# A decoder layer on one core: new instruction orders for start, middle and end, grouped moments, bias rows by TensorE

## The chip, the cores and the metric

One core of a Trainium2 chip. The time is that of one launch on the device in microseconds (us); the median of several runs counts. A profile of one execution gives the span from the first to the last instruction of the core and every instruction's start and duration.

## What is computed

One decoder layer over 32 batch items (here "batches") of 128 tokens and 128 features, 16 heads of 8. Cut to what matters:

```python
x = x + self_attn(layernorm(layernorm(x)) * ln_g + ln_b)   # scores + relative bias, softmax, @ w_out + b_out
x = x + cross_attn(layernorm(x), ctx, mask)                # masked softmax, @ Wo + bo
x = x + ffn(layernorm(x))   # y, h rounded to 8 bits per row, ternary weights; h = silu(gate) * up, then down
```

Scores need more accuracy than bf16 gives, so queries and keys are split into three bf16 parts each (their sum is the float), and the nine products stand as rows of one contraction.

## The kernel before, in words

The kernel is one program for five engines, each with its own list of instructions in fixed order; semaphores tie them together. There is no loop on the chip: Python runs a function `step` for t = -1 to 41 (`STEPS`, L41) and each call adds to every engine's list the instructions of that step. A helper such as `scores_a("X", st, 5, 1)` takes the stage (S self-attention, X cross-attention, F feed-forward), a lag and a chunk: in step t it works on batch t - 5, and does nothing if there is no such batch (`Step.of`). The order of the lines in each engine's `step` is the order of its work; one such list serves all 43 steps, and where work is missing at the start and the end, what is left keeps its place. `run(step)` (L216) drives it.

What happens to one batch, stage S:

- DVE: `ln_stats`, `ln_moments` (bn_stats, bn_aggr of x, L785 and L795), GpSimd (POOL): `variance`, `negate_mean`, `inverse_std`, `normalise` (L404 to L436) give xn.
- TensorE (PE): `xn_transposed`; ScalarE (ACT): `xnT_out`; PE: `project_qkv`; ACT: `qk_out` (the two bias columns), `part1`, `part2`, `v_out`; POOL: `rest`, `part3`. This makes the bf16 parts.
- SP's queue: `parts_again` and `parts_out` write the parts to a DRAM scratch, `stack_in` (L305, L308) reads them back as `stack_q` and `stack_k`, two buffers each (`STACKS`). For S the lower rows of the stack hold the relative bias; `rel_rows` (L235) fills them once for buffer 0, from ACT's queue for stack_k and SP's for stack_q, and `rel_copies` (L244) copies them to buffer 1. `scores_a` of batch 0 waits for the first, of batch 1 for the second.
- `scores_a` (PE, L1128) makes the scores in four chunks of four heads, in two PSUM banks; `row_max` (DVE; L900 for S, one reduction a chunk, L895 for X, four masked ones a chunk) takes the negated maxima; POOL splits them (`max_hi`, `max_lo`), PE transposes, ACT copies, and `max_in` (SP, L319) puts them as two more rows under `stack_q`.
- `scores_b` (PE, L1148) makes the transposed scores less the maximum, `exp` (ACT, L599) the probabilities, `attend` (PE, L1166) sums values and denominators; `o_raw_out`, `o_transposed`, `attend_sums`, `attend_norm` (DVE, L910, L920), `on_transposed`, `oT_out`, `project_out` (PE, L1245), `residual` (DVE, L930). Before that, POOL's `add_shift` (L458) has added the output bias row (with the values' bias carried through w_out) to x.

Stage X is the same with ctx as keys and values. Stage F: moments and xn on POOL as above, `y_max`, `y_unit`, `y_inverse` (DVE, L958), `quantise_y` (POOL), `y_transposed`, `yT_out`, `gate_up` (PE), `tanh` (ACT, L711), `gate` and `gated` (DVE, L965 and L975: h), `h_max`, `h_quantum`, `h_inverse`, `h_scaling`, `quantise_h` (ACT, L721), `h_transposed`, `hT_out` (ACT, L659), `down`, `residual_ffn` (L1027). Rounding adds 1536 in 16-bit floats; `yT_out` and `hT_out` take it off with a bias column.

PSUM banks are shared: bank_t by `o_transposed`, `gate_up`, `h_transposed`, `down`; bank_s by the small transposes and `project_out`; bank_p by `project_qkv` and `gate_up`; bank_o by `attend`. Who must have read a bank before it is written again stands by hand as arguments of each PE helper, as in

```python
scores_a("S", st, 2, 3, ("max_S", 2, 2), ("max_X", 6, 4), ("max_X", 6, 2), ("max_S", 3, 4))
```

SP's list also holds the bulk loads (`bulk_load`, L330 to L337): ctx and mask of four batches, and x of four batches two groups ahead, each 256 KB in a step of its own; x of batches 0 to 7 is loaded at the very start.

Of the kernel before, what the change touches and what calls it, by code (L numbers as in the profile page):

```python
# [16 lines left out]
CH = 4  # L28
HC = H // CH
# [11 lines left out]
STEPS = [(t, t) for t in range(-1, B + 10)]  # L41
# [4 lines left out]
CTX_TURN, MASK_TURN, X_TURN = 0, 2, 1  # L46

ONES, IDENT, V_AUG_S, POOL_CONST = 2, 5, 14, 17
SCALED, QK_BIAS, REL_SPLIT, V_BIAS, DVE_CONST = 1, 6, 12, 15, 17
ABS_SUM, MEAN_W, FFN_CONST = 1, 2, 15  # L50
# [7 lines left out]
class Step:  # L58


    def __init__(self, s, x):
        self.first = {"S": s, "X": x, "F": x}

    def of(self, stage, lag):

        first = self.first[stage]
        return first - lag if first is not None and 0 <= first - lag < B else None


START = Step(0, None)  # L70


def layer(nc, x, ctx, mask, w_self, w_cross, w_ffn, w_down, cols, w_out_s, w_out_x, bo_rows,
          rel_w, rel_const, scratch, scratch_rel, out):
    es = ExitStack()
    with es:
# [11 lines left out]
        w_tern = sb("w_tern", [D, 3, F], BF16)  # L88
        col = sb("col", [D, CONST_COLS])
        bo = sb("bo", [S, 2, D])  # L90
        shift = {"S": sb("shift_s", [S, D]), "X": sb("shift_x", [S, D])}
# [8 lines left out]
        round16 = sb("round16", [128, 1])  # L100
        minus_round16 = sb("minus_round16", [128, 1])
        y_step2 = sb("y_step2", [S, 1])
        minus_half = sb("minus_half", [128, 1])
# [22 lines left out]
        stats = {k: sb(f"stats_{k}", [S, 6]) for k in "SXF"}  # L126
        mv = {k: sb(f"mv_{k}", [S, 2]) for k in "SXF"}
        veps = {k: sb(f"veps_{k}", [S, 1]) for k in "SXF"}
        rstd = {k: sb(f"rstd_{k}", [S, 1]) for k in "SXF"}
# [8 lines left out]
        probs = {a: sb(f"probs_{a}", [S, CH, HC * S]) for a in "SX"}  # L138
        o_raw = {a: sb(f"o_raw_{a}", [128, 2, S]) for a in "SX"}
        neg_mean = {k: sb(f"neg_mean_{k}", [S, 1]) for k in "SXF"}  # L140
# [21 lines left out]
        hT = sb("hT", [128, CH, S], BF16)  # L162
# [6 lines left out]
        def quarter(bank, n):  # L169
# [7 lines left out]
            "rel_loaded qkv_loaded attn_loaded ffn_loaded x_loaded_first0 x_loaded_first1 x_loaded0 x_loaded1 ffn_const rel_out "  # L177
# [3 lines left out]
            "xn_X xn_F shifted_S shifted_X xnT_ps_S xnT_ps_X xnT_S xnT_X qkv_ps_S qkv_ps_X q_S q_X "  # L181
# [26 lines left out]
        def after(eng, st, *users):  # L208

            for name, lag, *signal in users:  # L210
                stage = name[-1] if name[-2:] in ("_S", "_X") else "F"
                b = st.of(stage, lag)
                if b is not None:
                    eng.wait_ge(sems[name], done(b, CH, signal[0]) if signal else done(b))
                    return

        def run(step):
            for s, x in STEPS:
                step(Step(s, x))
# [1165 lines left out]
```

## Time and profile before

| | us |
|---|---|
| runs shown | 459.56, 460.83, 462.85 (median 460.83) |
| span of the profiled execution | 457.5 |
| busy: PE, DVE, ACT, POOL | 398.0, 385.7, 359.9, 329.2 |
| stretch 200 to 250: PE, DVE, ACT, POOL | 48.91, 48.62, 46.65, 42.38 |

The profiled execution has no time but its span; the runs were timed without a profile, their median is 3.3 us above the span. An engine is busy from an instruction's start to its end, waiting for semaphores and issuing transfers left out. Matmuls are pipelined, so TensorE's share says little.

### The profile page before, as it was taken

To read this page: it belongs to the slowest core of one execution; us is meant where nothing else is said; L and a number is where in the kernel's file an instruction comes from. 1 tells how busy PE (TensorE), PEld (TensorE's weight loads), DVE (VectorE), ACT (ScalarE), POOL (GpSimd) and SP (SyncE) were. 2 spreads that over 40 slices of the span, in tenths; PEclk is the share of its full clock that TensorE was granted. 3 is DMA by queue.
4 is the path that set the end of the run, shared out by engine and by line. 5 is a ranking of instruction groups with operands and counts; after the bars stand their busy time and mean duration, and the time that the engine had idled before them with its cause. 6 is when DMAs were issued, how large, how long until landed. Compare 5 with 4: busy or idle time off the path is not lost. (4 is left out here: it accounts for less than half of the span.)

```text
span 457.5 us, 18022 instructions
## 1 busy us (share of the span) xinstructions
PE 398.0 (87%) x5405; PEld 311.5 (68%) x5436; DVE 385.7 (84%) x1920; ACT 359.9 (79%) x962; POOL 329.2 (72%) x917
## 2 busy tenths in 40 slices
PE   3267879999999999999999999999999999877762
PEld 2245657777777777777877777778877777654430
DVE  4645467999999999999999999999999999888532
ACT  2214758899999999999999999999999998865542
POOL 6834667888888888888888888888888765654120
PEclk9998999999999999999999999999999999998655
DMA  6654577756666766676657675676567662422100
GB/s 190 162 146 100 140 188 184 173 149 172 173 159 160 191 163 168 150 195 172 170 148 196 175 175 153 164 181 170 152 158 189 165 164 80 101 78 77 30 6 13
DMA packets 100181, 67.27 MB, mean 147 GB/s; under 512 B 73269, under 2 KB 90421, under 8 KB 100085
## 3 DMA queue, kind: packets, MB, share of 16 engines
q1 hardware_dynamic: 98209, 64.08, 54.7%
q10 hardware_dynamic: 1876, 2.03, 1.5%
q8 instruction: 45, 0.74, 0.7%
q14 instruction: 51, 0.42, 0.3%
HBM read 46.08 MB, written 19.07 MB: 142 GB/s over the span
## 5 line engine op out<-in xcount | busy, mean ns | idle before, releaser
L895 DVE CUSTOM_DVE_ANT_0 biased<-bank,mask_bias 128x128 bf16<-128x128 f32 x512 | 112.8, 285 | 4.0 <-PE bank L1128 3.9
L900 DVE TENSOR_REDUCE neg_max_S<-bank 128x4 f32<-128x512 f32 x128 | 85.4, 675 | 21.1 <-PE bank L1128 20.4
L599 ACT ACTIVATE probs_S<-bank 128x512 f32<-128x512 f32 x128 | 72.7, 597 | 11.0 <-PE bank L1148 11.0
L599 ACT ACTIVATE probs_X<-bank 128x512 f32<-128x512 f32 x128 | 72.5, 590 | 7.0 <-PE bank L1148 6.4
L1128 PE MATMUL bank<-stack_k_S,stack_q_S 120*128 120x128 bf16 x512 | 50.5, 223 | 11.7 <-DMA stack_k_S<-scratch_S 11.0
L1148 PEld LDWEIGHTS bank<-stack_q_X,stack_k_X 74*128 74x128 bf16 x512 | 41.1, 100 | 16.6 <-issue 2.1
L1128 PEld LDWEIGHTS bank<-stack_k_S,stack_q_S 120*128 120x128 bf16 x512 | 38.6, 102 | 20.1 <-issue 11.9
L1148 PE MATMUL bank<-stack_q_X,stack_k_X 74*128 74x128 bf16 x512 | 51.4, 224 | 0.0
L1145 PE MATMUL bank<-ident_bf,mask_bias 128*128 128x512 bf16 x128 | 50.6, 396 | 0.0
L1128 PE MATMUL bank<-stack_k_X,stack_q_X 72*128 72x128 bf16 x512 | 45.3, 221 | 2.9 <-DMA stack_k_X<-scratch_X 1.7
L1166 PE MATMUL bank<-probs_X,v_aug_X 128*32 128x128 f32 x1024 | 42.4, 285 | 0.0
L895 DVE DVE_READ_ACCUMULATOR2_ANT neg_max_X<- 128x1 f32 x512 | 42.3, 83 | 0.0
L1148 PE MATMUL bank<-stack_q_S,stack_k_S 122*128 122x128 bf16 x512 | 40.5, 222 | 0.1
L1148 PEld LDWEIGHTS bank<-stack_q_S,stack_k_S 122*128 122x128 bf16 x512 | 34.0, 102 | 7.9 <-issue 6.7
L404 POOL TENSOR_SCALAR veps_F<-mv_F 128x1 f32<-128x1 f32 x32 | 6.1, 192 | 41.6 <-DVE mv_F L795 41.6
L1128 PEld LDWEIGHTS bank<-stack_k_X,stack_q_X 72*128 72x128 bf16 x512 | 32.1, 98 | 5.8 <-DVE neg_max_S L900 3.7
L1166 PE MATMUL bank<-probs_S,v_aug_S 128*32 128x128 f32 x1024 | 34.8, 276 | 0.0
L1166 PEld LDWEIGHTS bank<-probs_X,v_aug_X 128*32 128x32 f32 x1024 | 24.6, 111 | 9.9 <-ACT probs_X L599 2.9
L965 DVE SCALAR_TENSOR_TENSOR h_gate<-tanh_g,bank 128x512 f32<-128x512 f32 x32 | 21.7, 680 | 11.1 <-ACT tanh_g L711 11.1
L721 ACT ACTIVATE h_q<-h,round,h_scale 128x512 f16<-128x512 f32 x32 | 26.7, 833 | 4.4 <-DVE h_scale L1019 4.4
L1166 PEld LDWEIGHTS bank<-probs_S,v_aug_S 128*32 128x32 f32 x1024 | 25.9, 109 | 4.2 <-ACT probs_S L599 0.3
L632 ACT ACTIVATE qk_S<-bank,qk_bias_s 128x128 f32<-128x128 f32 x64 | 20.0, 363 | 8.5 <-PE bank L1219 7.8
(165 smaller groups left out, 1178.6 us busy)
## 6 DMA issues: line engine op xcount, KB each, us to landing
stack_q_S<-scratch_S SPq DMA_DIRECT2D x32, 288.0 KB
stack_k_S<-scratch_S SPq DMA_DIRECT2D x32, 288.0 KB
stack_q_X<-scratch_X SPq DMA_DIRECT2D x32, 288.0 KB
stack_k_X<-scratch_X SPq DMA_DIRECT2D x32, 288.0 KB
scratch_S<-qk_parts_S SPq DMA_DIRECT2D x32, 192.0 KB, 2.7
scratch_X<-qk_parts_X SPq DMA_DIRECT2D x32, 192.0 KB, 2.7
scratch_S<-qk_parts_S SPq DMA_DIRECT2D x32, 64.0 KB, 1.7
ctxT<-ctx SPq DMA_DIRECT2D x8, 256.0 KB, 4.7
```

Of the source, the lines that this page charges most:

```text
L404: pool.tensor_scalar(veps[k][:], mv[k][:, 1:2], scale, offset, ALU.mult, ALU.add)\
L599: act.activation(probs[a][:, c, :], bank_b[c % 2][:, :], ACT.Exp).then_inc(sems["exp_" + a], 1)
L632: act.activation(qk[a][:, m, :], quarter(bank_p, m), ACT.Identity, bias=qk_bias[a][:, m:m + 1], scale=(HD ** -0.5, 1.0)[m]).then_inc(sems[ ...
L721: act.activation(h_q[:], h[:], ACT.Identity, bias=round16[:, 0:1], scale=h_scale[:, 0:1])\
L895: last = dve.tensor_tensor_reduce(biased[:, c, hh, :], quarter(bank_a[c % 2], hh), mask_bias[:, b % 2, :], -1.0, -2.0 * BIG, ALU.add, ALU.min,
L900: dve.tensor_reduce(neg_max[a][:, first_head(c):first_head(c) + 2 * HC - 1:2], bank_a[c % 2][:, :].rearrange("i (h j) -> i h j", h=HC), AX ...
L965: dve.scalar_tensor_tensor(h_gate[:], tanh_g[:], 1.0, bank_t[:, :], ALU.add, ALU.mult)\
L1128: last = pe.matmul(bank[:, part_of_bank(hh)], stack_q[a][rows, b % STACKS, head(c, hh)], stack_k[a][rows, b % STACKS, head(c, hh)], start= ...
L1145: pe.matmul(bank[:, :], mask_bias[:, b % 2, :], ident_bf[:].unsqueeze(1).to_broadcast([S, HC, S]), start=True, stop=False)
L1148: last = pe.matmul(bank[:, part_of_bank(hh)], stack_k[a][rows, b % STACKS, head(c, hh)], stack_q[a][rows, b % STACKS, head(c, hh)], start= ...
L1166: last = pe.matmul(bank_o[32 * hh:32 * hh + 32, half * S:(half + 1) * S], v, probs[a][:, c, part_of_bank(hh)], start=u == 0, stop=u == 1, ...
```

## The change

Every helper keeps its arithmetic but for four edits; all lists of instructions are new.

1. *Three orders.* `fill` for s = -1 to 1, `step` for x = 0 to 32 (with s = x + 2), `drain` for the rest, one of each per engine. A helper works on all batches that are due and not yet begun (`Step.due`), so that lags may differ between the three. PE keeps account of who last held a bank (`take`) instead of the lists by hand.
2. *Moments of x in groups* of 1, 3 and then 4 batches: bn_stats and bn_aggr per batch as before, but in one go; variance, negated mean and power once per group. x loads have a semaphore each and `load_x` issues them early.
3. *Bias rows by TensorE*: the row is split into three bf16 rows, and a second product with ones adds it in PSUM; `add_shift` goes.
4. *h transposed copied as 32-bit words*, without subtraction: `down` gets a fifth product that takes off 1536 times the weights' sum. Its weights are 16-bit floats instead of bf16.

Beside these: `probs` is doubled, so exp waits for attend of two batches before; `yT_out` and `quantise_h` take a constant in place of a bias column.

```diff
-STEPS = [(t, t) for t in range(-1, B + 10)]
+LEAD, TAIL, LAGS = 2, 3, 12
+MOMENTS = (0, 1, 4, 8, 12, 16, 20, 24, 28, 32)
...
+    def due(self, stage, lag, *key, n=B):
+        if self.newest[stage] is None:
+            return range(0)
+        first = self.begun.get((stage, key), 0)
+        end = max(first, min(self.newest[stage] - lag + 1, n))
+        self.begun[stage, key] = end
+        return range(first, end)
...
+        def run(begun, fill, step, drain):
+            for s in range(-1, LEAD):
+                fill(Step(s, None, begun))
+            for x in range(B + TAIL - LEAD):
+                step(Step(x + LEAD, x, begun))
+            for x in range(B + TAIL - LEAD, B + TAIL + LAGS):
+                drain(Step(x + LEAD, x, begun))
...
@@ SP @@
-                store(st, 10)
-                parts_again("S", st, 0)
-                parts_out("S", st, 0)
-                rel_rows(sp, st, 0, stack_q)
-                rel_copies(sp, st, 0)
-                stack_in("X", st, 4)
-                max_in("X", st, 5)
-                stack_in("S", st, 0)
-                bulk_load(st, 0)
-                parts_again("X", st, 3)
-                parts_out("X", st, 3)
-                max_in("S", st, 1)
+            def fill(st):
+                stack_in("S", st, 0)
+                max_in("S", st, 1)
+                load_c(st, -2)
+                load_x(st, -2)
+                parts_again("S", st, -1)
+                parts_out("S", st, -1)
+                if st.at(0):
+                    rel_rows(sp, stack_q)
+                if st.at(1):
+                    rel_copies(sp)
+            def step(st):
+                load_c(st, 1)
+                stack_in("S", st, 0)
+                store(st, 18)
+                parts_again("X", st, 2)
+                parts_out("X", st, 2)
+                max_in("S", st, 1)
+                load_x(st, -2)
+                stack_in("X", st, 2)
+                parts_out("S", st, -1)
+                max_in("X", st, 3)
+                parts_again("S", st, -1)
...
@@ ACT, end of fill; hT_out @@
+                part2("S", st, -1)
+                if st.at(0):
+                    rel_rows(act, stack_k)
...
-                act.activation(hT[:].rearrange("p c s -> p (c s)"), bank_t[:, 0:256].bitcast(F16), ACT.Identity,
-                               bias=minus_round16[:, 0:1]).then_inc(sems["hT"], 1)
+                    copy(hT[:].rearrange("p c s -> p (c s)").bitcast(F32), bank_t[:, 0:256]).then_inc(sems["hT"], 1)
...
@@ DVE, step @@
+                row_max("S", st, 1, 3)
+                ln_moments("X", st, 1)
+                residual_ffn(st, 6)
+                row_max("X", st, 3, 0)
+                attend_sums("S", st, 2)
+                y_max(st, 5)
+                attend_norm("S", st, 2)
+                y_unit(st, 5)
+                y_inverse(st, 5)
+                row_max("X", st, 3, 1)
+                row_max("X", st, 3, 2)
+                row_max("X", st, 3, 3)
+                ternary_weights(st, 1)
+                residual("S", st, 2)
+                ln_group(st, -3)
+                gate(st, 5)
+                gated(st, 5)
+                attend_sums("X", st, 4)
+                attend_norm("X", st, 4)
+                h_max(st, 5)
+                row_max("S", st, 0, 0)
+                h_quantum(st, 5)
+                h_inverse(st, 5)
+                out_scaling(st, 5)
+                h_scaling(st, 5)
+                residual("X", st, 4)
+                row_max("S", st, 0, 1)
+                ln_stats("F", st, 4)
+                ln_moments("F", st, 4)
+                ln_stats("X", st, 0)
+                row_max("S", st, 0, 2)
...
@@ DVE, drain: its last lines @@
+                gate(st, 5)
+                attend_sums("X", st, 4)
+                ln_stats("X", st, -12)
+                attend_norm("X", st, 4)
+                gated(st, 5)
+                h_max(st, 5)
...
@@ PE, step: from the scores that end a batch of X to the output product of S @@
+                attend("X", st, 4, 0)
+                scores_a("X", st, 3, 2)
+                y_transposed(st, 5)
+                scores_b("X", st, 4, 3)
+                scores_a("X", st, 3, 3)
+                gate_up(st, 5)
+                project_out("S", st, 2)
...
-                pe.matmul(quarter(bank_s, 2), oT[a][:], w_o[a][:], start=True, stop=True)\
+                    pe.matmul(quarter(bank_s, 2), oT[a][:], w_o[a][:], start=True, stop=False)
+                    pe.matmul(quarter(bank_s, 2), ones_bf[:], shift_rows3[:, "SX".index(a), :], start=False, stop=True)\
...
+                        pe.matmul(bank_t[:, 256:384], hT[:, c, :], w_down16[:, c * 128:(c + 1) * 128],
+                                  start=c == 0, stop=False)
+                    last = pe.matmul(bank_t[:, 256:384], minus_offset[:], w_down_sum[:], start=False, stop=True)
```

In ACT's `step`, `yT_out(5)` stands behind the third `exp` of X, then `part1` of S, the fourth `exp` of X and `tanh(5)`.

## Rows read from the trace of the kernel before

**Rows 1.** Stretches: us; busy us (count) PE PEld DVE ACT POOL; PEclk, DMA, GB/s
```profile
20.00:40.00 20.00, 11.79 (x103) 8.31 (x103) 8.29 (x17) 6.17 (x19) 6.50 (x17) 1.00 0.59 151
...
200.00:250.00 50.00, 48.91 (x709) 39.51 (x712) 48.62 (x258) 46.65 (x130) 42.38 (x119) 1.00 0.66 172
...
440.00:457.50 17.50, 5.70 (x24) 2.57 (x24) 6.62 (x23) 4.33 (x7) 2.44 (x9) 0.50 0.03 8
```

**Rows 2.** Timeline of DVE (start us, us): product h of batches 0, 24, 31
```profile
87.61 0.69 DVE L975 TENSOR_TENSOR h<-h_gate,bank 128x512 f32<-128x512 f32 x1
...
371.19 0.69 DVE L975 TENSOR_TENSOR h<-h_gate,bank 128x512 f32<-128x512 f32 x1
...
450.22 0.69 DVE L975 TENSOR_TENSOR h<-h_gate,bank 128x512 f32<-128x512 f32 x1
```

**Rows 3.** Groups, 120 to 360 us, DVE: busy us, mean ns, idle before
```profile
L895 DVE CUSTOM_DVE_ANT_0 biased<-bank,mask_bias 128x128 bf16<-128x128 f32 x326 | 71.8, 285 | 0.1
...
L900 DVE TENSOR_REDUCE neg_max_S<-bank 128x4 f32<-128x512 f32 x81 | 54.3, 673 | 0.4
```

**Rows 4.** Timeline of DVE: residual additions and the instruction behind each
```profile
204.16 0.29 DVE L930 TENSOR_TENSOR x_all<-bank,x_all 128x128 f32<-128x128 f32 x1
204.37 0.17 DVE L795 BATCH_NORM_AGGREGATE mv_S<-stats_S 128x2 f32<-128x6 f32 x1
...
209.00 0.28 DVE L930 TENSOR_TENSOR x_all<-bank,x_all 128x128 f32<-128x128 f32 x1
209.32 0.29 DVE L785 BATCH_NORM_STATS2 stats_F<-x_all 128x6 f32<-128x128 f32 x1
```

**Rows 5.** Groups, 120 to 360 us, the engines that lose or gain work
```profile
L458 POOL TENSOR_TENSOR x_all<-x_all,shift_x 128x128 f32<-128x128 f32 x20 | 9.2, 460 | 0.0
...
L424 POOL TENSOR_TENSOR rstd_S<-veps_S,minus_half 128x1 f32<-128x1 f32 x20 | 11.5, 575 | 0.0
...
L659 ACT ACTIVATE hT<-bank,minus_round 128x512 bf16<-128x512 f16 x20 | 13.7, 687 | 0.0
...
L602 ACT ACTIVATE o_raw_X<-bank 128x256 f32<-128x256 f32 x21 | 8.1, 384 | 7.6 <-PE bank L1166 7.6
...
L1191 PE MATMUL bank<-ident_bf,neg_max_parts_S 128*128 128x128 bf16 x20 | 4.4, 219 | 0.0
```

**Rows 6.** Timeline of DVE: y_inv to gate, in the middle and in batch 31
```profile
201.21 0.10 DVE L958 RECIPROCAL y_inv<-y_step 128x1 f32<-128x1 f32 x1
...
205.50 0.68 DVE L965 SCALAR_TENSOR_TENSOR h_gate<-tanh_g,bank 128x512 f32<-128x512 f32 x1
...
446.27 0.16 DVE L958 RECIPROCAL y_inv<-y_step 128x1 f32<-128x1 f32 x1
...
449.50 0.69 DVE L965 SCALAR_TENSOR_TENSOR h_gate<-tanh_g,bank 128x512 f32<-128x512 f32 x1 [3.07 <-ACT tanh_g L711]
```

**Rows 7.** Timeline of the start: issues of transfers by ScalarE and SP
```profile
13.79 1.29 ACTq L235 DMA_DIRECT2D stack_k_S<-scratch_rel  x3
...
14.47 1.91 SPq L235 DMA_DIRECT2D stack_q_S<-scratch_rel  x3
...
17.06 0.81 SPq L305 DMA_DIRECT2D stack_q_S<-scratch_S  x1
...
29.22 0.71 SPq L319 DMA_DIRECT2D stack_q_S<-neg_maxT_S  x1
```

**Rows 8.** Timeline: first scores of batches 0, 1; maxima of batches 2, 7
```profile
24.11 1.01 PE L1128 MATMUL bank<-stack_k_S,stack_q_S 120*128 120x128 bf16 x8 [6.79 <-DMA stack_k_S<-scratch_S]
...
31.27 0.58 PE L1128 MATMUL bank<-stack_k_S,stack_q_S 120*128 120x128 bf16 x4 [2.51 <-DMA stack_k_S<-scratch_S]
...
43.11 0.67 DVE L900 TENSOR_REDUCE neg_max_S<-bank 128x4 f32<-128x512 f32 x1
...
98.14 0.67 DVE L900 TENSOR_REDUCE neg_max_S<-bank 128x4 f32<-128x512 f32 x1
```

**Rows 9.** Timeline of DVE: gate of batch 30
```profile
438.84 0.69 DVE L965 SCALAR_TENSOR_TENSOR h_gate<-tanh_g,bank 128x512 f32<-128x512 f32 x1 [4.13 <-ACT tanh_g L711]
```

More of the change, by code:

```diff
@@ L760, in _ @@
+                part1("X", st, 3)
+                qk_out("X", 1, st, -15)
+                v_out("X", st, -15)
+                tanh(st, 7)
+                o_raw_out("X", st, 6)
+                maxT_out("X", st, 5)
+            run(begun, fill, step, drain)
         @block.vector
@@ new lines, in scores_b @@
+            def scores_b(a, st, lag, c):
+                for b in st.due(a, lag, "scores_b", c):
+                    bank, rows = bank_b[c % 2], slice(0, A_ROWS[a] + M_ROWS)
+                    take(f"b{c % 2}", ("exp_" + a, done(b, CH, c + 1)))
+                    if c == 0 and a == "S" and b < WARM_BATCHES:
+                        keep_warm(bank)
+                    if c == 0:
+                        pe.wait_ge(sems[f"max_in_{a}{b % STACKS}"], loaded(b, 16))
+                    masked = a == "X"
+                    if masked:
+                        pe.matmul(bank[:, :], mask_bias[:, b % 2, :], ident_bf[:].unsqueeze(1).to_broadcast([S, HC, S]),
+                                  start=True, stop=False)
+                    for hh in range(HC):
+                        last = pe.matmul(bank[:, part_of_bank(hh)], stack_k[a][rows, b % STACKS, head(c, hh)],
+                                         stack_q[a][rows, b % STACKS, head(c, hh)], start=not masked,
+                                         stop=not masked or hh == HC - 1)
+                    last.then_inc(sems["score_b_" + a], 1)
@@ new lines, in attend @@
+            def attend(a, st, lag, c):
+                for b in st.due(a, lag, "attend", c):
+                    pe.wait_ge(sems["exp_" + a], done(b, CH, c + 1))
+                    if c == 0:
+                        if a == "S" and b == 0:
+                            pe.wait_ge(sems["dve_const"], QK_BIAS)
+                        pe.wait_ge(sems["v_" + a], done(b))
+                        take("o", ("o_raw_" + a, done(b)))
+                    half, u = divmod(c, 2)
+                    for hh in range(HC):
+                        v = v_aug[a][:, b % V_COPIES, HC * half + hh, 2 * u:2 * u + 2, :].rearrange("s b e -> s (b e)")
+                        last = pe.matmul(bank_o[32 * hh:32 * hh + 32, half * S:(half + 1) * S], v,
+                                         probs[a][:, b % 2, c, part_of_bank(hh)], start=u == 0, stop=u == 1,
+                                         skip_group_check=True)
+                    last.then_inc(sems["av_" + a], 1)
@@ L1337 @@
+            run(begun, fill, step, drain)
 _OUT = ((B, S, D), "float32")
```

1550 lines of the change are left out of this document (755 added, 795 removed).

## The prediction

> **What bounds the kernel now.** I read the busy shares by stretch first. From 200 to 250 us [rows 1] VectorE (DVE) is busy 48.62 of 50 us, 97%; ScalarE 46.65, GpSimd 42.38. TensorE's 48.91 is no limit: its matmuls overlap, and eight in a row take 1.01 us [rows 8], not eight times the 219 ns of one [rows 5]. From 20 to 40 us no engine is half busy but TensorE, and in the last 17.5 us DVE works 6.6. So there are three stretches with different limits: a start that waits, a middle that DVE fills, an end that waits again.
>
> Second, the pace. The product that makes h (L975) runs once per batch: 87.61 for batch 0, 371.19 for batch 24, 450.22 for batch 31 [rows 2]. The middle takes 283.6 / 24 = 11.82 us a batch, the end 79.0 / 7 = 11.3, though self-attention is over there. After batch 31's h another 457.5 - 450.2 = 7.3 us follow.
>
> Third, how much of DVE's 11.82 is work. Per batch, sixteen masked maxima (mean 285 ns) and four plain ones (673 ns) are the largest pieces [rows 3]. 3% idle is 0.35 us a batch. More is hidden, because busy counts a whole instruction and its tail may lie under the next one: after a residual add at 204.16 the next instruction starts 0.21 us later, after the one at 209.00 it takes 0.32 [rows 4], and no idle time is noted. Laying the start-to-start distances of such tight pairs over one batch, I estimate 11.2 us of work that can't shrink. DVE has 0.35 to 0.6 us to give back per batch, and no more, since the change takes no instruction from it in the middle.
>
> **The change part by part.**
>
> *Work taken off other engines.* GpSimd loses two shift additions of 0.46 us, and of self-attention's variance, negated mean and power three quarters (the power alone is 0.575 us) [rows 5]: about 0.92 + 0.75 = 1.7 us of the 42.38 / 50 x 11.82 = 10.0 us per batch. ScalarE's copy of h transposed handles 256 words instead of 512: 687 ns become about 384, as a 256-word copy from PSUM takes [rows 5]; 0.3 us. Constants in place of bias columns on two other activations: between -0.3 and +0.3 us each, the difference of that same pair of rows; I take 0, since ScalarE does not set the pace. TensorE gains two bf16 products per batch for the bias rows and one for h's offset: 219 ns each if alone [rows 5], some 0.06 in a row, so 0.17 to 0.66 us. In the middle all this is cover, not time: none of it is DVE's. It would cost if DVE waited for project_out; then the upper bound is 0.66 x 24 = 16 us, the lower 0; I take 0.
>
> *The middle order.* I walked DVE's new list against the others' with these durations. Almost every DVE item has its input before its turn. The tight place is the feed-forward chain: y_inverse, quantise_y, y_transposed, yT_out, gate_up, tanh, gate. In the kernel before, DVE does 4.3 us of other work between y_inv (201.21) and gate (205.50). In the new list twelve masked maxima (71.8 us for 326 is 0.22 each [rows 3]), one residual addition and, one step in four, the grouped moments lie between: about 3.0 us. The chain unobstructed, in the last batch, takes 449.50 - 446.27 = 3.2 us [rows 6], at the 1.2 GHz level (granted clock 0.50 [rows 1]); I estimate its TensorE pieces 0.5 us shorter at 2.4 GHz, so 2.7. That fits by 0.3 us. Bounds per batch: 11.2 (nothing late) and 11.8 (as now). I take 11.3: 24 x (11.82 - 11.3) = -12.5 us; the ends are -15 and 0. The grouped moments are as many instructions as before, bunched in one step of four; that step's gate comes about 1 us later and the other three gain it. Doubling probs lets exp run without attend of the batch before; no row shows ScalarE waiting for that, so 0.
>
> *The start.* Here the SP queue decides. Before: the bias rows of stack_q go out at 14.47, batch 0's stack at 17.06, ScalarE's bias rows at 13.79 [rows 7], first scores at 24.11, batch 1's at 31.27 [rows 8]. In the new order all six x loads lie in the first five steps, and three loads of 256 KB (one of ctx, two of x) go ahead of batch 0's parts. At the 151 GB/s of the second stretch [rows 1] 0.79 MB is 5 us; I take 4, since the queue is then empty of the bias rows. The bias rows for stack_q come after batch 0's stack, a mask load, an x load and batch 1's parts: about 17.06 + 4 = 21 for the stack, 24.5 for the bias rows, landing near 30. Scores of batch 0 then start at 30, not 24.1 (bounds 26 and 32). The copies of the bias rows to the second stack, right after the first ones before, now stand behind max_in of batch 0, which went out at 29.22 [rows 7], 5.1 us after batch 0's scores. So they go out near 37 behind batch 2's parts; with 4 us to land (the stack needed up to 7, from 17.06 to 24.11) batch 1's scores start near 41, against 31.27. From there the steps should be faster than before: from batch 2's maxima at 43.11 to batch 7's at 98.14 [rows 8] a batch took 11.0 us, with engines half idle; from batch 0's scores to batch 1's it took 7.2. These are my bounds; cross-attention joins on the way, so I take 9.5, nearer to the upper. Batch 7's maxima: 41 + 6 x 9.5 = 98, as before. But the new order is one step deeper: gate of batch 0 now stands just ahead of batch 7's first maxima, where it stood just behind batch 6's. The new constants on DVE (six to split the bias rows, two for the offset's sum) lie where it is busy 8.29 of 20 us [rows 1]: 0, without that cover some 2 us. h of batch 0 comes at about 97, not 87.6: +9. Bounds: +3 (steps of 8.5 instead of 9.5) and +15 (steps of 10.5).
>
> A rule of the skill speaks against this part. The trace has batch 0's stack issued at 17.06 and its scores 7 us later [rows 7, 8], with other transfers on the same queue. The Trainium skill, DMA: Bandwidth & Descriptors, section "Queues, rings and completion order", says that each DMA engine takes the descriptors of one queue in ring order. By it the parts wait for the whole 0.79 MB, which gives the 4 us taken above; if the engines shared instead, first scores would be late by 2 us rather than 6 and the start would cost about +5.
>
> *The end.* After self-attention's last maxima the new order has one more step to go than the old (seven, not six), already in the +9. Its own order drops the stand-ins for missing work. One cycle there is gate, attend, output product, residual, moments, y, gate; before it took 449.50 - 438.84 = 10.66 us [rows 6, 9] for the last batch, all of it a chain. The new order moves gated behind attend_norm and shortens little else on it: 10.15 a step at the low clock, 10.4 to 10.8 in the three steps where self-attention runs out. 11.3 + 10.8 + 10.6 + 10.4 + 3 x 10.15 = 73.5 instead of 79.0: -5.5 (bounds: -10 if the chain runs at full clock, and 0). After the last h: -0.3 by the short copy.
>
> **Sum.** 457.5 + 9 - 12.5 - 5.5 - 0.3 = 448.2 us of span. The median of the runs shown, 460.83, is 3.3 above that span; the same 3.3 on top gives 451.5.
>
> **The rivals.**
> 1. *The start costs little.* +3 there, the middle at its floor (-15), the end -7: span 438.2, time 441.5. For it: engines sit half idle from 20 to 40 us. Against: the order of SP's issues is there to read.
> 2. *The start eats it.* +15 there, -9 in the middle, -5 at the end, -0.3: 458.2, time 461.5, no change. For it: the in-order SP queue, with the bias copies behind batch 0's maxima. Against: the steps after it have little work.
> 3. *DVE stops at gate (slower).* The chain from y_inverse to gate has 0.3 us of room; TensorE has scores and attend of other batches in front of gate_up, ScalarE three exp in front of tanh. If these make tanh 1.1 us late in each step, DVE waits 0.8 and the period is 12.1: +6.7 in the middle, +9 at the start, -4 at the end: 469.2, time 472.5. It turns the sign from a wait of about 0.5 us per batch on. For it: the room is thin, 0.3 us where the old order had 4.3 - 2.7 = 1.6. Against: by the rows each of those pieces is through before its turn.
>
> **How the numbers follow.** The forecast (446 to 457) has 0.45, rival 1 0.18, rival 2 0.21, rival 3 0.16. About 1% (4.6 us) is what a measurement of this kernel can tell from no change. Faster by over 1% (under 456.2): most of the forecast, 0.41, rival 1, and 0.02 of rival 2: 0.61. Within 1%: 0.04 and 0.18 of rival 2: 0.22. Slower: 0.01 of rival 2 and rival 3: 0.17. The range takes in rival 1 nearly whole and rival 2, and leaves out most of rival 3: 439 to 465; the forecast's own is 446 to 457.
>
> **What would show it.** Start: the first scores near 30 us and batch 1's near 41; batch 0's h near 97. Middle: h every 11.3 us, DVE's share above 98%, hardly any wait of gate for tanh. End: seven steps of 10 to 11 us. The forecast is wrong if h comes every 11.8 or more in the middle (look for DVE waiting for tanh or for project_out), or if batch 0's h comes later than 103.

## The result and the profile after

The changed kernel takes 517.05 us (median of 4 runs, 516.4 to 521.75), the kernel before took 461.43 us beside it: a ratio of 1.123, with a 95% interval of 1.118 to 1.127. The prediction was 451.5 us and its range ended at 465. The profiled execution of the changed kernel has a span of 514.3 us against 457.5, that is 56.8 us more. Some executions of a kernel here took over 1.5% longer than its fastest: the ratios below are taken over the others, the medians over all.

The timeline of DVE in the changed kernel has the product that makes h in line 1006. These are batches 0, 24 and 31:

```profile
109.88 0.69 DVE L1006 TENSOR_TENSOR h<-h_gate,bank 128x512 f32<-128x512 f32 x1
...
424.91 0.69 DVE L1006 TENSOR_TENSOR h<-h_gate,bank 128x512 f32<-128x512 f32 x1
...
507.20 0.69 DVE L1006 TENSOR_TENSOR h<-h_gate,bank 128x512 f32<-128x512 f32 x1
```

Against [rows 2] the start is 109.9 - 87.6 = 22.3 us longer, the 24 batches of the middle (424.9 - 109.9) - 283.6 = 31.4 us, the end 82.3 - 79.0 = 3.3 us, and what follows the last h 0.2 us shorter (7.1 for 7.3). A batch in the middle takes 315.0 / 24 = 13.13 us, not 11.82 and not the predicted 11.3. In what follows "period" and "batch 0's h" are read in this way from each run's trace.

The first two stretches of [rows 1] in the changed kernel, busy time by engine (PE, PEld, DVE, ACT, POOL), then granted clock, DMA share, GB/s:

```profile
20.00:40.00 20.00, 6.72 (x36) 4.38 (x36) 8.50 (x22) 3.21 (x10) 7.41 (x13) 1.00 0.53 143
200.00:250.00 50.00, 45.27 (x660) 38.29 (x664) 42.54 (x222) 41.54 (x119) 31.50 (x88) 0.97 0.55 147
```

From 20 to 40 us TensorE does 6.7 us for 11.8. In the middle every engine that computes works less than before: DVE 42.5 of 50 us for 48.6, GpSimd 31.5 for 42.4. None of them is the limit. The table leaves out SP, which only issues transfers and is never counted as busy. Its own waits, from 150 to 400 us (total, times, longest), say more. Before:

```profile
SPq L279 <- ACT qk_parts_X L602: 43.4, 21, 4.1
SPq L319 <- ACT neg_maxT_X L602: 20.8, 21, 1.5
...
SPq L300 <- DMA scratch_X<-qk_parts_X: 2.2, 2, 1.4
```

After:

```profile
SPq L295 <- DMA scratch_X<-qk_parts_X: 52.5, 20, 3.8
SPq L295 <- DMA scratch_S<-qk_parts_S: 41.4, 19, 3.6
SPq L300 <- DMA scratch_S<-qk_parts_S: 8.4, 19, 1.5
SPq L285 <- POOL qk_parts_X L491: 2.6, 4, 1.1
```

Before, SP waits for its producers: ScalarE has not yet made the parts or the maxima. After, it waits for its own transfers: 52.5 + 41.4 + 8.4 = 102.3 us in 250 / 13.13 = 19 steps, 5.4 us in each, for the landing of the parts in scratch (the moment when the whole transfer has arrived) before it can load the stack from there. The kernel before spent 2.2 us on that in all. For its producers SP waits 91.6 us before and 3.7 us after (all such lines of the two views added up): after, its own issues and landings fill its step. One step of SP shows where. Timeline of SP in the kernel before (start, duration of the issue):

```profile
250.32 0.36 SPq L279 DMA_DIRECT2D scratch_S<-qk_parts_S  x1
251.07 0.36 SPq L288 DMA_DIRECT2D scratch_S<-qk_parts_S  x1
251.54 0.79 SPq L305 DMA_DIRECT2D stack_q_X<-scratch_X  x1
252.37 0.76 SPq L308 DMA_DIRECT2D stack_k_X<-scratch_X  x1
254.32 0.69 SPq L319 DMA_DIRECT2D stack_q_X<-neg_maxT_X  x1
255.18 0.77 SPq L305 DMA_DIRECT2D stack_q_S<-scratch_S  x1
```

And in the changed kernel, from one load of self-attention's stack to the next:

```profile
258.09 0.79 SPq L300 DMA_DIRECT2D stack_q_S<-scratch_S  x1
258.93 0.76 SPq L303 DMA_DIRECT2D stack_k_S<-scratch_S  x1
259.78 1.06 SPq L278 DMA_DIRECT2D scratch_X<-qk_parts_X  x1
260.93 0.42 SPq L285 DMA_DIRECT2D scratch_X<-qk_parts_X  x1
261.47 0.70 SPq L312 DMA_DIRECT2D stack_q_S<-neg_maxT_S  x1
264.68 0.78 SPq L300 DMA_DIRECT2D stack_q_X<-scratch_X  x1
265.82 0.75 SPq L303 DMA_DIRECT2D stack_k_X<-scratch_X  x1
266.69 0.44 SPq L285 DMA_DIRECT2D scratch_S<-qk_parts_S  x1
267.23 0.71 SPq L312 DMA_DIRECT2D stack_q_X<-neg_maxT_X  x1
268.04 0.40 SPq L278 DMA_DIRECT2D scratch_S<-qk_parts_S  x1
271.84 0.79 SPq L300 DMA_DIRECT2D stack_q_S<-scratch_S  x1
```

Before, the other attention's stack load and maxima stand between a write to scratch (250.32, 251.07) and the load of the same parts (255.18): the landing is over by then. After, the load of a stack is the next item, or the next but one, behind the last write of its own parts. SP stands still from 262.17 to 264.68 for X and from 268.44 to 271.84 for S, 2.51 + 3.40 us; the other 7.84 us of this 13.75 us step are its issues and short gaps between them. Nothing else fits into the two waits, since SP takes its list in order.

The landing has become longer too. Transfers of the page, KB each, median us from the start of the issue to the landing, in the changed kernel (parts_out writes the 192 KB, L285, parts_again the 64 KB, L278):

```profile
scratch_S<-qk_parts_S SPq DMA_DIRECT2D x32, 192.0 KB, 4.1
scratch_X<-qk_parts_X SPq DMA_DIRECT2D x32, 192.0 KB, 3.7
...
scratch_S<-qk_parts_S SPq DMA_DIRECT2D x32, 64.0 KB, 3.3
```

In the kernel before:

```profile
scratch_S<-qk_parts_S SPq DMA_DIRECT2D x32, 192.0 KB, 2.7
scratch_X<-qk_parts_X SPq DMA_DIRECT2D x32, 192.0 KB, 2.7
scratch_S<-qk_parts_S SPq DMA_DIRECT2D x32, 64.0 KB, 1.7
```

The writes now follow a stack load of 2 x 288 KB by less than a microsecond (259.78 behind 258.93). What the rest of the kernel sees are late maxima above all. Three of the longest waits of all engines, 150 to 400 us:

```profile
DVE inv_sum_X L956 <- PE bank L1234: 29.2, 17, 4.1
PE bank L1206 <- DMA stack_q_S<-neg_maxT_S: 28.2, 17, 4.1
ACT probs_S L634 <- PE bank L1206: 27.9, 17, 4.1
```

TensorE waits 28.2 / 17 = 1.7 us at a time for self-attention's maxima, which SP brings, and ScalarE's exp and DVE wait behind it. That gate waits for tanh, the slower rival of the prediction, stands nowhere in the list of waits of this stretch.

### The profile page after: what moved, and what is told of

It reads as the page before. It is cut to its first block and busy times, and to the rows that moved or that the text cites. A ratio compares the mean times of both kernels' runs of the same rounds, so it can differ in the third digit from the quotient of the medians.

```text
span 514.3 us, 18102 instructions
## 1 busy us (share of the span) xinstructions
PE 400.9 (78%) x5501; PEld 322.8 (63%) x5532; DVE 382.4 (74%) x1928; ACT 348.0 (68%) x962; POOL 282.7 (55%) x784
## 5 line engine op out<-in xcount | busy, mean ns | idle before, releaser
L943 DVE CUSTOM_DVE_ANT_0 biased<-bank,mask_bias 128x128 bf16<-128x128 f32 x512 | 115.2, 285 | 11.0 <-PE bank L1188 8.8
L948 DVE TENSOR_REDUCE neg_max_S<-bank 128x4 f32<-128x512 f32 x128 | 84.4, 681 | 28.2 <-PE bank L1188 27.9
L634 ACT ACTIVATE probs_X<-bank 128x512 f32<-128x512 f32 x128 | 75.0, 587 | 21.5 <-PE bank L1206 21.3
L1206 PE MATMUL bank<-stack_q_S,stack_k_S 122*128 122x128 bf16 x512 | 50.1, 236 | 44.5 <-DMA stack_q_S<-neg_maxT_S 43.9
L1188 PE MATMUL bank<-stack_k_S,stack_q_S 120*128 120x128 bf16 x512 | 49.2, 233 | 17.2 <-DMA stack_q_S<-scratch_rel 12.7
L1188 PE MATMUL bank<-stack_k_X,stack_q_X 72*128 72x128 bf16 x512 | 51.3, 224 | 5.0 <-DMA stack_k_X<-scratch_X 4.8
L1188 PEld LDWEIGHTS bank<-stack_k_X,stack_q_X 72*128 72x128 bf16 x512 | 34.0, 100 | 12.5 <-issue 7.8
L956 DVE RECIPROCAL inv_sum_X<-bank 128x16 f32<-128x16 f32 x32 | 8.2, 257 | 43.3 <-PE bank L1234 43.3
L484 POOL TENSOR_TENSOR qk_rest_X<-qk_X,qk_parts_X 128x256 f32<-128x256 f32 x32 | 21.5, 672 | 14.0 <-ACT qk_parts_X L637 13.9
L732 ACT ACTIVATE h_q<-h,h_scale 128x512 f16<-128x512 f32 x32 | 23.1, 721 | 8.7 <-DVE h_scale L1040 7.8
```

The lines of the kernel that those rows point to most:

```text
L484: pool.tensor_tensor(qk_rest[a][:], qk[a][:], qk_parts[a][:, b % 2, :, 0, :], ALU.subtract)\
L634: act.activation(probs[a][:, b % 2, c, :], bank_b[c % 2][:, :], ACT.Exp).then_inc(sems["exp_" + a], 1)
L732: act.activation(h_q[:], h[:], ACT.Copy, bias=ROUND16, scale=h_scale[:, 0:1])\
L943: last = dve.tensor_tensor_reduce(biased[:, c, hh, :], quarter(bank_a[c % 2], hh), mask_bias[:, b % 2, :], -1.0, -2.0 * BIG, ALU.add, ALU.min,
L948: dve.tensor_reduce(neg_max[a][:, first_head(c):first_head(c) + 2 * HC - 1:2], bank_a[c % 2][:, :].rearrange("i (h j) -> i h j", h=HC), AX ...
L956: dve.reciprocal(inv_sum[a][:], o[:, :, HD]).then_inc(sems["inv_sum_" + a], 1)
```

## The experiments

Theory 1: SP's in-order list bounds the middle, by two landings in series per step. Theory 2: TensorE's new order does. Theory 3: the new arithmetic does. Theory 4, for the start: the order of the first transfers. All times are medians; the kernel before took 458.8 to 461.4 us beside them. Batch 0's h, period and the column b24 to b31 come from one trace each.

| run | us | ratio to before (95%) | batch 0's h | period | b24 to b31 |
|---|---|---|---|---|---|
| changed kernel | 517.05 | 1.118 to 1.127 | 109.9 | 13.13 | 82.3 |
| e8: before, landings exposed | 515.84 | 1.117 to 1.130 | 94.5 | 13.85 | 77.6 |
| e1: changed, SP interleaved | 531.45 | none | 110.2 | 14.05 | 79.8 |
| e2: changed, PE's scores later | 525.48 | 1.137 to 1.149 | 113.0 | 13.34 | 80.6 |
| e5: changed, start mended | 511.25 | none | 103.9 | 13.19 | 79.2 |
| e9: changed, one write earlier | 509.97 | 1.103 to 1.124 | 111.0 | 12.68 | 83.9 |
| e10: changed, repaired | 484.22 | 1.044 to 1.055 | 99.8 | 12.45 | 76.3 |
| e12: e10 with the change's SP list | 506.26 | 1.096 to 1.110 | 100.1 | 13.15 | 79.4 |
| e3: arithmetic alone | 467.82 | 1.013 to 1.027 | 92.0 | 12.04 | 77.3 |
| e4: and moments early | 470.12 | 1.009 to 1.024 | 97.7 | 11.81 | 78.0 |
| e13: and no added products | 469.86 | 1.015 to 1.028 | 99.5 | 11.83 | 81.6 |
| e14: e4, shift on GpSimd | 468.40 | 1.017 to 1.026 | 96.9 | 11.79 | 78.7 |
| e11: e3, nine items moved | 470.62 | 1.018 to 1.025 | 88.8 | 12.28 | 79.9 |

**e8: the suspected cause put into the kernel before.** In SP's list alone, cross-attention's stack load and its maxima now stand ahead of self-attention's writes:

```diff
                 store(st, 10)
-                parts_again("S", st, 0)
-                parts_out("S", st, 0)
-                rel_rows(sp, st, 0, stack_q)
-                rel_copies(sp, st, 0)
                 stack_in("X", st, 4)
                 max_in("X", st, 5)
+                parts_again("S", st, 0)
+                parts_out("S", st, 0)
+                rel_rows(sp, st, 0, stack_q)
+                rel_copies(sp, st, 0)
                 stack_in("S", st, 0)
```

> The kernel before with one edit: SyncE loads cross-attention's stack and its maxima ahead of writing out self-attention's parts, so that each load of a stack directly follows the write to scratch that it waits for, as in the changed kernel. Nothing else is changed, no arithmetic and no other engine's order. Theory 1: the period rises from 11.82 to 12.6 to 13.2 us, the time from 461 to 480 to 500 us. Theories 2 and 3: time within 5 us of 461.

Measured: 515.84 us, period 13.85. With not one operation changed, this order costs as much as the whole change, and more than expected. SP's waits, 150 to 400 us:

```profile
SPq L300 <- DMA scratch_X<-qk_parts_X: 53.3, 18, 4.2
SPq L300 <- DMA scratch_S<-qk_parts_S: 51.3, 18, 4.0
```

104.6 us in 18 steps, 5.8 us each: the pattern of the changed kernel. The landings grew with it, those of the 192 KB writes from 2.7 us to 3.2 (S) and 4.2 (X). Exposed landings on SP are enough to cause a loss of this size; theories 2 and 3 aren't needed for it.

**e1: SP's list alone mended in the changed kernel.**

```diff
                 max_in("S", st, 1)
                 load_x(st, -2)
-                stack_in("X", st, 2)
-                parts_out("S", st, -1)
-                max_in("X", st, 3)
                 parts_again("S", st, -1)
+                parts_out("S", st, -1)
+                stack_in("X", st, 2)
+                max_in("X", st, 3)
```

> The changed kernel with only SyncE's middle order changed: the parts of self-attention are written out before cross-attention's stack is loaded, so that a whole stage of other issues lies between each write to scratch and the load that waits for it. Theory 1 (SyncE's in-order queue waits for two scratch landings in series in each step, 2.5 to 3.8 us each): the period falls from 13.1 to about 11.5 us, batch 0's h comes some 6 us earlier than 109.9, the time is about 517 - 24 x 1.6 - 6 - 3 = 470 us (465 to 480). Theory 2 (TensorE's order) and theory 3 (the new arithmetic costs time): the period stays at 13.0 to 13.2 and the time within 3 us of 517.

Measured: 531.45 us (521.26 to 536.46; the runs scatter and no ratio is given), period 14.05. The expectation failed in all four runs. The trace is that of the longest (536.46 us), so part of the 14.05 may be this execution's alone. SP's waits in it, 150 to 400 us:

```profile
SPq L278 <- ACT qk_parts_S L637: 54.4, 18, 4.8
SPq L312 <- ACT neg_maxT_S L637: 31.0, 15, 4.8
...
SPq L295 <- DMA scratch_S<-qk_parts_S: 0.9, 2, 0.8
```

The landings are covered (0.9 us), but cross-attention's stack now stands behind self-attention's parts, which the other engines make late in this kernel's step: 54.4 us of waiting for them took the place of the landings. SP's list mended alone does not help, since the other four lists were made for its old order; e10, below, moves them with it. In this execution TensorE also lost its clock behind a wait (two neighbouring stretches, columns as above, and the matmul that ends the wait):

```profile
260.00:280.00 20.00, 18.04 (x272) 14.68 (x274) 17.03 (x99) 16.25 (x47) 13.20 (x40) 1.00 0.58 142
280.00:300.00 20.00, 15.95 (x185) 12.86 (x183) 12.36 (x60) 11.85 (x35) 9.17 (x25) 0.74 0.42 100
```

```profile
288.34 0.59 PE L1188 MATMUL bank<-stack_k_X,stack_q_X 72*128 72x128 bf16 x4 [3.83 <-DMA stack_k_X<-scratch_X]
```

**e2: TensorE's order.** The scores that wait for the maxima go behind four items that don't:

```diff
-                scores_b("S", st, 1, 0)
-                scores_b("S", st, 1, 1)
                 scores_a("S", st, 0, 0)
                 o_transposed("X", st, 4)
                 xn_transposed("X", st, 1)
                 max_transposed("X", st, 3)
+                scores_b("S", st, 1, 0)
+                scores_b("S", st, 1, 1)
                 scores_b("S", st, 1, 2)
```

> The changed kernel with only TensorE's middle order changed: the first two groups of self-attention's second scores stand behind four other stages, so that waiting for their maxima holds up less. Theory 2 (TensorE's order, work queued behind these scores): the period falls by 1 us or more, time under 490 us. Theory 1 (SyncE's queue): the wait only moves, period 12.9 to 13.2, time 510 to 520 us.

Measured: 525.48 us (three runs 523.02 to 527.48, one 674.68), period 13.34. Theory 2 expected a shorter period and gets none from this order; both numbers lie a little above what theory 1 gave. With e8 beside it, TensorE's 28.2 us of waiting for the maxima read as a symptom.

**e9: a smaller dose.**

```diff
                 max_in("S", st, 1)
+                parts_again("S", st, -1)
                 load_x(st, -2)
                 stack_in("X", st, 2)
                 parts_out("S", st, -1)
                 max_in("X", st, 3)
-                parts_again("S", st, -1)
```

> The changed kernel with one SyncE item moved: the smaller write of self-attention's parts goes out while SyncE would wait for cross-attention's landing, so that the last write ahead of the next stack load leaves about 1 us earlier; both landings are still waited for in series. Theory 1 (the step is the sum of SyncE's issues and of two landings): the period falls by what is taken out of that sum, 0.6 to 1.2 us, to 11.9 to 12.5, time 488 to 502 us. A rival, that the middle hangs on the longest chain from projection to scores and not on SyncE's sum: self-attention's parts are ready before, so nothing is gained, period 12.9 to 13.2, time 512 to 520 us.

Measured: 509.97 us, period 12.68. The middle gains 0.44 us a batch, in the direction of theory 1 and against the rival, but below the expected 0.6 to 1.2; the time lies between the two expectations (488 to 502, 512 to 520). Part of what the landings gave up became waiting for ScalarE's parts of S, 29.1 us from 150 to 400 us. The intervals of the two ratios overlap (1.103 to 1.124 against 1.118 to 1.127), so the gain is read from the one trace.

**e10 and e12: the change repaired, and SP's list put back.** e10 has SP's middle list interleaved, the mended start of e5, and eighteen items of the other four middle lists moved by one to eight places. e12 differs from it in SP's middle list alone:

```diff
+                load_c(st, 1)
                 stack_in("S", st, 0)
+                store(st, 18)
                 parts_again("X", st, 2)
                 parts_out("X", st, 2)
                 max_in("S", st, 1)
-                load_c(st, 2)
-                store(st, 18)
-                parts_again("S", st, -1)
-                parts_out("S", st, -1)
+                load_x(st, -2)
                 stack_in("X", st, 2)
-                load_x(st, -2)
+                parts_out("S", st, -1)
                 max_in("X", st, 3)
+                parts_again("S", st, -1)
```

Of the other lists' moves, these are some of ScalarE's (e10 against the changed kernel):

```diff
-                v_out("X", st, 2)
-                quantise_h(st, 6)
                 qk_out("X", 1, st, 2)
-                xnT_out("S", st, -1)
+                quantise_h(st, 6)
+                v_out("X", st, 2)
                 part1("X", st, 2)
+                xnT_out("S", st, -1)
...
+                part1("S", st, -1)
...
                 yT_out(st, 5)
-                part1("S", st, -1)
                 exp("X", st, 4, 3)
```

> The changed kernel with SyncE's interleaved middle order, the mended start, and on the other engines a few items of the middle moved by one to four places, so that what SyncE waits for (self-attention's parts, the maxima) is made earlier in the step; lags, buffers and arithmetic are the changed kernel's. Theory 1 (SyncE's landings, and, once they are covered, the chain from the parts to SyncE through the other engines): period 11.6 to 12.4 us, time 455 to 480 us. If the shorter pipeline itself can't hold the pace, whatever the order: period 12.8 or more, time over 490 us.

> The repaired changed kernel (its mended start and the moved items of the other four engines) with SyncE's middle list put back to that of the change. Theory 1 (SyncE's two landings in series set the step): the period goes back to 12.8 to 13.4 us and the time to 498 to 515 us, whatever the other engines do. Rival (the other engines' moves were what helped): period 12.3 to 12.6, time 480 to 488 us.

Measured: e10 484.22 us, period 12.45, both just above theory 1's ranges for it (455 to 480, 11.6 to 12.4) and well below the rival's; e12 506.26 us, period 13.15, both inside theory 1's. Batch 0's h is the same in both (99.8 and 100.1), so the 22 us between them belong to SP's list in the middle and at the end. SP's waits in e12, then in e10:

```profile
SPq L295 <- DMA scratch_X<-qk_parts_X: 53.6, 19, 3.9
SPq L295 <- DMA scratch_S<-qk_parts_S: 44.6, 19, 4.3
SPq L300 <- DMA scratch_S<-qk_parts_S: 8.3, 19, 1.0
```

```profile
SPq L285 <- POOL qk_parts_S L491: 26.8, 20, 1.6
SPq L285 <- POOL qk_parts_X L491: 24.6, 20, 1.3
...
SPq L295 <- DMA scratch_S<-qk_parts_S: 1.9, 4, 0.7
```

With SP's list of the change the other engines' moves help the middle nothing (13.15 against 13.13); with landings covered they bring it to 12.45. Theory 1 holds for this half of the middle's loss, with a rider: SP's list and its producers have to be mended together.

**e5: the start.** The bias rows go out behind batch 0's parts, their copies at the head of their step, ctx, mask and x behind the parts (SP's fill list, shown, and ScalarE's, whose bias rows likewise go from `st.at(0)` to `st.at(-1)`):

```diff
             def fill(st):
+                if st.at(1):
+                    rel_copies(sp)
                 stack_in("S", st, 0)
                 max_in("S", st, 1)
-                load_c(st, -2)
-                load_x(st, -2)
                 parts_again("S", st, -1)
                 parts_out("S", st, -1)
-                if st.at(0):
+                if st.at(-1):
                     rel_rows(sp, stack_q)
-                if st.at(1):
-                    rel_copies(sp)
+                load_c(st, -2)
+                load_x(st, -2)
```

> The changed kernel with only the start's order mended: the bias rows go out behind batch 0's parts, their copies at the head of their step, and the bulk loads of ctx, mask and x behind the parts. Theory 4 (the order of these transfers costs the start 6 us at the first scores and 12 us at batch 1's): first scores at 24 to 26 us, batch 1's at 31 to 34, the time some 8 to 10 us shorter, 507 to 509 us. Theory 1 alone (the pace from batch 4 on is set by the middle's loop of SyncE, whatever came before): a shift of what comes before carries through just the same, so 505 to 510 us; if instead the start is bound by its steps of 9 us, the gain is under 3 us.

Measured: 511.25 us (504.62 to 514.56), batch 0's h at 103.9: 6.0 us earlier, and kept to the end. But the first scores came at 29.4, not 24 to 26, and batch 1's at 37.3, not 31 to 34 (43.3 in the changed kernel): this order costs the start 6 us, not the 8 to 10 that were put on it.

**e3, e4, e13, e14: arithmetic and moments in the orders of the kernel before.** Each keeps that kernel's lists. e3 has the new arithmetic, with moments in groups one step of four; e4 takes all moments in the first eight steps, as the changed kernel does; e13 leaves TensorE's three added products out of e4 (so the biases and the offset are missing from its result); e14 is e4 with the bias rows on GpSimd again and x loaded from ScalarE's queue. SP's list of the kernel before as it stands in all four (e14 has no load_x there), and the lines that e13 drops from e4:

```diff
-                bulk_load(st, 0)
+                load_c(st, 0)
+                load_x(st, 0)
...
-                    pe.matmul(quarter(bank_s, 2), ones_bf[:], shift_rows3[:, "SX".index(a), :], start=False, stop=True)\
...
-                    last = pe.matmul(bank_t[:, 256:384], minus_offset[:], w_down_sum[:], start=False, stop=True)
```

> The arithmetic of the change without its orders: every engine keeps the order of the kernel before (one list for all steps, SyncE's x loads one step of four as there); the bias rows are a TensorE product, self-attention's moments are taken in groups of four one step of four, h transposed is copied as 32-bit words, down has its fifth product, the constants are immediates, probs has two buffers. Theory 1 (the loss is SyncE's new order and nothing else): period 11.6 to 11.9 us, batch 0's h at 86 to 92, time 453 to 463 us. Theory 3 (the new arithmetic costs time in the middle, 1.3 us a batch): period near 13, time over 485 us.

> As the run with the arithmetic alone, with one difference: all of self-attention's moments are taken in the first eight steps and SyncE loads x one group a step, as in the changed kernel. DVE then has two instructions less per batch in the middle, 0.3 us by their start-to-start distances (0.20 and 0.10). If DVE's work bounds the middle: period 12.04 - 0.3 = 11.7 us, and the start 3 to 10 us later for the early loads; time 460 to 466 us. If a chain through other engines bounds it: period 11.95 to 12.1 and time 466 to 474 us.

> The run with early moments without TensorE's three added products per batch (the two for the bias rows and the fifth of down): the biases of both attentions' outputs and the offset of the down product are left out of the result. In that run TensorE is busy 49.1 to 49.6 of 50 us and DVE 47.6 to 48.0. If TensorE's list bounds the middle: 0.2 to 0.35 us a batch less, period 11.45 to 11.6, time 460 to 465 us. If these products are hidden, as the prediction had it: period 11.75 to 11.85, time 468 to 472 us.

> A version meant to keep what helped: the lists of the kernel before, bias rows added by GpSimd as before (no bias product on TensorE), self-attention's moments taken in the first eight steps in groups, x loaded one group a step from ScalarE's queue and not from SyncE's, h transposed as 32-bit words. If the 0.3 us of DVE and the 0.2 to 0.3 us of TensorE per batch are real gains against the runs so far: period 11.4 to 11.6, start 88 to 93, time 450 to 458 us. If the middle hangs on a chain that neither touches: period 11.8, time 459 to 466 us.

Measured periods: 12.04, 11.81, 11.83, 11.79. e3 refutes theory 3 (13 expected by it), though its 467.82 us and 12.04 lie above the 453 to 463 and 11.6 to 11.9 that theory 1 gave: the arithmetic with this placement costs 4.4 us at the start and 0.22 x 24 = 5.3 in the middle. e4 gets the 0.22 back, where 0.3 was expected if DVE's work bounds the middle and nothing if a chain does, and pays 5.7 at the start. e13 shows that the added products are hidden, as the prediction had it. e14 misses its ranges (11.79 is the chain's 11.8, but 468.40 us lie above its 459 to 466); it has neither x's loads on SP's queue nor the six added constants on DVE, and its start is only 0.8 us shorter than e4's, so these two aren't what makes e4's start long. The stretch 200 to 250 us of e4, then of e13:

```profile
200.00:250.00 50.00, 49.14 (x724) 39.55 (x717) 47.64 (x250) 44.76 (x127) 35.09 (x100) 1.00 0.63 162
```

```profile
200.00:250.00 50.00, 48.93 (x714) 39.33 (x712) 47.86 (x254) 45.18 (x130) 35.38 (x99) 1.00 0.64 162
```

In both DVE works 0.8 to 1.0 us less than in [rows 1] and the period stays at 11.8, that of the kernel before: here less work on DVE, or on TensorE, did not bring it lower. What holds it at 11.8 stays open.

**e11: an attempt at a better version.** e3 with eight items moved on four lists; one of them, on DVE:

```diff
+                row_max("S", st, 2, 1)
...
-                row_max("S", st, 2, 1)
```

> The run with the arithmetic alone (one list for all steps, the orders of the kernel before) with nine items moved: on SyncE the bulk loads, on ScalarE xnT_out and on TensorE xn_transposed of self-attention earlier in the step, on DVE h_scaling later and row_max S 1 earlier, on TensorE two score groups. From the waits of the arithmetic-alone run: 5 us at the start (batch 0's h at 92.0 against 87.6) and up to 0.3 us a batch are to be had: 452 to 462 us. If the middle is DVE's own work, nothing but the start: 461 to 465 us.

Measured: 470.62 us, above both expectations. The start gained 3.2 us against e3 (88.8 for 92.0), the middle lost 0.24 a batch (12.28). No version here beats the kernel before.

## Why the prediction was wrong

**The middle: -12.5 predicted, +31.4 measured.** The step that failed is the one under the middle order: "I walked DVE's new list against the others' with these durations. Almost every DVE item has its input before its turn." The walk had no time on SP's list, though the prediction read SP's order closely for the start. The term that it put at nothing is the wait of a stack load for the landing of its own parts, measured at 5.4 us a step; with the 13.13 - 5.4 = 7.7 us of issues and gaps it makes the step. The landings of the kernel before would not have told it: X's last write at 260.93 would land 2.7 us later, 1.5 us after the maxima's issue, S's at 268.04 after 1.7, 1.3 us behind its issue. I estimate from these rows 7.7 + 2.8 = 10.5 us, less than the 11.8 of a step. It takes the landings of 3.3 to 4.1 us, behind a stack load on the same queue, to reach 13.1. e8 shows that the order of SP suffices, the pair e12 and e10 that it is worth 0.70 us a batch in the changed kernel. Of its 1.31 us a batch over the kernel before, the other 0.6 (12.45 against e4's 11.81) stayed in e10, the one order tried with SP and its producers mended; that the shorter pipeline causes them is not shown.

The predicted gain would not have come either. "DVE has 0.35 to 0.6 us to give back" read 97% busy as a floor near 11.2. In e4, e13 and e14 DVE is busy about 0.2 us less per batch than before, GpSimd is lighter as well (35.1 to 38.6 of 50 us for 42.4), and the period is 11.8. And "as many instructions as before, bunched in one step of four" was a misreading of the list: the changed kernel takes one group a step, the last moments of all 32 batches at 81.8 us, so that the middle has none.

**The start: +9 predicted, +22.3 measured.** The working held up to batch 1's scores. First scores and batch 1's, in the changed kernel:

```profile
30.75 1.04 PE L1188 MATMUL bank<-stack_k_S,stack_q_S 120*128 120x128 bf16 x8 [12.71 <-DMA stack_q_S<-scratch_rel]
...
43.30 0.58 PE L1188 MATMUL bank<-stack_k_S,stack_q_S 120*128 120x128 bf16 x4 [4.10 <-issue]
```

30 and 41 were forecast, and the bracket names the bias rows. Partly this was luck: batch 0's stack was issued at 19.75, 2.7 us later than before and not 4, and the bias rows, issued at 23.64 for 24.5, took 7.1 us to the scores and not 5.5. The term that failed is the steps after it, "so I take 9.5", against rows that showed 11.0. Maxima of batches 1, 4 and 7:

```profile
43.98 0.69 DVE L948 TENSOR_REDUCE neg_max_S<-bank 128x4 f32<-128x512 f32 x1 [7.42 <-PE bank L1188]
...
71.88 0.69 DVE L948 TENSOR_REDUCE neg_max_S<-bank 128x4 f32<-128x512 f32 x1 [0.94 <-PE bank L1188]
...
111.61 0.68 DVE L948 TENSOR_REDUCE neg_max_S<-bank 128x4 f32<-128x512 f32 x1
```

To batch 4 a step took 27.9 / 3 = 9.3 us, as taken; from there, with cross-attention joining, 39.7 / 3 = 13.2. That these three steps are the middle's loop on SP is not shown: e12, with this SP list, takes 12.3 a step for them, e10, without it, 12.4, and batch 0's h is the same in both. Of the 22.3 us, e5 shows 6.0 for the order of transfers, and e4 has 10.1 with the old lists: 4.4 that e3 has too, and 5.7 with the moments and x's loads early. For early moments the prediction's start has no term (its "0, without that cover some 2 us" is for the new constants alone). That the 6.0 and the 10.1 add up was not tried, and how the two parts of the 10.1 arise stays open.

**The end: -5.5 predicted, +3.3 measured.** Its first three steps still run on the middle's lists and took 37.1 us for the 32.7 taken; e10, with SP's list mended, has 32.8 there and e12, with it put back, 34.5, so SP is part of it. Of the four steps on the new order the first two took 13.7 and 13.2, not 10.4 and 10.15 (12.5 and 12.7 in e10, so most of it is not SP's middle list and stays open), the last two 9.85 and 8.49, less than the 10.15 taken. **The tail** was -0.3 and is -0.2.

**The rivals.** The second had the right part, "the in-order SP queue", and the wrong place: start only. Its 461.5 is 55.6 us off, the forecast 65.6. The third, gate waiting for tanh, had the sign but not the wait (and by the prediction's own sum, 457.5 - 448.2 = 9.3 us, the sign turns at 0.39 us a batch, not at 0.5). The rule weighed there, the Trainium skill's DMA: Bandwidth & Descriptors, section Queues, rings and completion order (an engine takes the descriptors of one queue in ring order), agrees with the landings seen here: 192 KB writes issued right behind a 576 KB stack load land after 3.7 to 4.1 us, after 2.7 in the kernel before and 2.3 to 2.9 in e10, where they don't follow one so closely. It was weighed for the first scores and not applied to the middle.

## What to carry to other kernels

Walk the list of the engine that issues the transfers like any other: sum its issues per step, and add each landing that it waits for right behind its own write, at the length that it has in its new place: behind a big load of the same queue it was 3.3 to 4.1 us here, not 1.7 to 2.7. A write to scratch and the load that reads it want other work between them; in the kernel before, the load came 3.2 us (X) and 4.1 us (S) behind the last write in the step shown. When the order of one engine is mended, read the waits again: what its items wait for has its own place in the other lists, and the wait may only change its name (e1).

## What the runs showed of the hardware that was not expected

A queue engine that no busy share counts can be the limit: SP's issues took 0.40 to 1.06 us each in the step shown, and 5.4 us of each 13.1 us step went by in waits for landings, at a DMA share of 0.55. The landing of a 192 KB write went from 2.7 to 4.1 us by its place behind a load, at a lower total rate (147 GB/s for 172 in [rows 1]). And a wait can cost twice: in e1's longest run TensorE stood still for 3.83 us before 288.34, and its granted clock was 0.50 from 288 to 296, the lower of its two levels (1.2 and 2.4 GHz), where four matmuls of cross-attention's scores took 0.63 us for the 0.39 before the wait; from 300 to 304 it was 1.00 again. Not every wait did this (one of 1.44 us before 273.09 left it at 1.00), and the kernel before held 1.00 through [rows 1]'s middle.
